# A node tile's eleven transposes put into one run on TensorE, between the products of n and those of z

## What is computed

```python
h = layernorm(x)
gi = segment_sum(edge_mlp(h[src], edge_attr), dst) @ W_ih.T + b_ih     # per node, from the edge stage
gh = h @ W_hh.T + b_hh                                                # 512 -> 3 * 512: r, z, n
r = sigmoid(i_r + h_r); z = sigmoid(i_z + h_z)
n = tanh(i_n + r * h_n)
h_new = (1 - z) * n + z * h
x1 = x + h + batchnorm(h_new)
h2 = layernorm(x1)
f1 = h2 @ [Wg, W1 of 8 experts, Ws1] + biases                         # gate logits and hidden rows
hid = weight of the expert (0 unless in the top 2) * relu(f1)         # and the shared expert's
out = x1 + hid @ [W2, Ws2, biases]
```

## Time and profile before

| what | value |
|---|---|
| three runs | 1561.29, 1565.93, 1567.96 us, median 1565.93 |
| profiled execution | 1564.22 us, of which the span from first to last instruction is 1562.4 |
| TensorE busy | 1414.7 us, 91% of the span, 6780 products and transposes |
| VectorE busy | 1119.8 us, 72% |
| GpSimd busy | 935.3 us, 60% |
| ScalarE busy | 608.9 us, 39% |
| mean granted TensorE clock | 0.965 of full speed |

### The profile page before, as it was taken

One profiled execution on the slowest core, in us unless ns is written; L12 is line 12 of the kernel. 1 busy time (PEld: TensorE's weight loads), 2 busy tenths in 40 slices (PEclk: granted clock), 3 DMA queues, 4 the chain that ended last, 5 costly groups with the idle time before them and its releaser, 6 DMA issues. The chain is left out here.

```text
span 1562.4 us, 23252 instructions
## 1 busy us (share of the span) xinstructions
PE 1414.7 (91%) x6780; PEld 1143.0 (73%) x6780; DVE 1119.8 (72%) x2860; ACT 608.9 (39%) x1100; POOL 935.3 (60%) x1055
## 2 busy tenths in 40 slices
PE   4879988998355999999999999999999999999996
PEld 3658766786244787888888888788888888888884
DVE  4654333333124888888888888888888888888886
ACT  3421212112002444444444444444444444444442
POOL 3212221311116777778788777788777778877771
PEclk9979999999777999999999999999999999999998
DMA  6432243537432232233322222222222322232220
GB/s 184 161 142 74 59 109 69 119 78 190 114 86 78 88 100 94 98 99 100 101 95 96 93 94 94 95 94 97 97 98 98 98 98 98 98 98 98 96 85 30
DMA packets 77727, 156.00 MB, mean 100 GB/s; under 512 B 35937, under 2 KB 37839, under 8 KB 77569
## 3 DMA queue, kind: packets, MB, share of 16 engines
q0 software_dynamic: 45056, 79.03, 17.6%
q1 hardware_dynamic: 32638, 76.55, 15.1%
HBM read 103.38 MB, written 52.02 MB: 99 GB/s over the span
## 5 line engine op out<-in xcount | busy, mean ns | idle before, releaser
L1385 PE MATMUL bank<-whh_hi,h_hi 128*125 128x512 f32 x960 | 393.0, 409 | 31.4 <-DVE h_lo L480 31.4
L1385 PE MATMUL bank<-whh_hi,h_lo 128*125 128x512 f32 x960 | 380.7, 397 | 0.0
L1385 PE MATMUL bank<-whh_lo,h_hi 128*125 128x512 f32 x960 | 379.7, 395 | 0.0
L1385 PEld LDWEIGHTS bank<-whh_hi,h_hi 128*125 128x125 f32 x960 | 178.6, 186 | 69.8 <-DVE h_lo L480 31.8
L1385 PEld LDWEIGHTS bank<-whh_hi,h_lo 128*125 128x125 f32 x960 | 178.6, 186 | 45.3
L1385 PEld LDWEIGHTS bank<-whh_lo,h_hi 128*125 128x125 f32 x960 | 179.4, 187 | 38.1
L1152 POOL DMA_INDIRECT gates<-gates_in,slot_at x80 | 128.0, 1600 | 77.6 <-POOL slot_at L1150 69.4
L1239 ACT ACTIVATE hn_raw<-bank 125x512 f32<-125x512 f32 x80 | 47.8, 598 | 288.3 <-PE bank L1385 288.3
L1086 PE MATMUL bank<-wih_hi,a_hi 128*125 128x512 f32 x240 | 101.8, 424 | 49.7 <-DVE g_out L834 41.6
L506 POOL DMA_INDIRECT gates_in<-g_out,add_at x16 | 32.3, 2018 | 190.9 <-DVE g_out L834 111.8
L834 DVE SCALAR_TENSOR_TENSOR g_out<-ig_bias,is_first,bank 125x512 f32<-125x512 f32 x60 | 44.5, 746 | 135.6 <-PE bank L1086 78.7
(11 more groups left out here) (174 smaller groups left out, 3330.8 us busy)
## 6 DMA issues: line engine op xcount, KB each, us to landing
xt<-in_x SPq DMA_DIRECT2D x80, 250.0 KB
out<-y SPq DMA_DIRECT2D x80, 250.0 KB
gates_in<-g_out SPq DMA_DIRECT2D x20, 750.0 KB
gates_in<-ig_bias SPq DMA_DIRECT2D x5, 750.0 KB
wih_lo_raw<-in_wih_t SPq DMA_DIRECT2D x4, 768.0 KB, 11.0
whh_lo_raw<-in_whh_t SPq DMA_DIRECT2D x4, 768.0 KB, 15.4
gates<-gates_in,slot_at POOLq DMA_INDIRECT x80, 10.8
m_lo_raw<-in_attr_t SPq DMA_DIRECT2D x5, 250.0 KB, 5.2
```

Of the source, the lines that this page charges most:

```text
L1385: last = pe.matmul(to[0:R, :], a[:, s, k * R:(k + 1) * R], w[:, k, q * D:(q + 1) * D], start=n == 0, stop=n == 3 * DK - 1)
```

## The change

On TensorE the transposes of h2 and of hid move ahead of those of h, and all eleven stand between the last product of n and the first of z. The products of z are no longer split. On ScalarE the copy h_hi moves behind h2_hi and hid_hi, which is the new order of the transposes. Nothing else changes; counts of instructions are the same.

```diff
@@ scalar body
                     act.activation(r_gate[:, :], r_pre[:, :], ACT.Sigmoid).then_inc(r_done, 1)
-                if p.has(1):
-                    s = p.slot(1)
-                    act.wait_ge(h_turned, t + 2)
-                    wait_from(act, z_prod, t)
-                    act.activation(h_hi[:, s, :], b_th[:, 0:DK * R], ACT.Copy).then_inc(h_hi_done, 1)
                 if p.has(-1):
                     act.wait_ge(h2_turned, t)
...
                     act.activation(hid_hi[:, :], b_thid[:, 0:KF * R], ACT.Copy).then_inc(hid_hi_done, 1)
+                if p.has(1):
+                    s = p.slot(1)
+                    act.wait_ge(h_turned, t + 2)
+                    wait_from(act, z_prod, t)
+                    act.activation(h_hi[:, s, :], b_th[:, 0:DK * R], ACT.Copy).then_inc(h_hi_done, 1)
@@ tensor body
                     gate(s, b_n, 2).then_inc(n_prod, 1)
+                if p.has(-1):
+                    pe.wait_ge(h2_done, t)
+                    wait_from(pe, h2_lo_done, t - 1)
+                    turn(pe, b_th2, h2[:, p.slot(-1), :], DK).then_inc(h2_turned, 1)
+                if p.has(-2):
+                    pe.wait_ge(hid_done, t - 1)
+                    wait_from(pe, hid_lo_done, t - 2)
+                    turn(pe, b_thid, hid[:, p.slot(-2), :], KF).then_inc(hid_turned, 1)
                 if p.has(1) and not p.first(1):
                     turn_h(pe, p)
                 if p.has(0):
                     wait_from(pe, z_pre_done, t)
-                    gate(p.slot(0), b_z, 1, 0, 2)
-                if p.has(-1):
-                    pe.wait_ge(h2_done, t)
-                    wait_from(pe, h2_lo_done, t - 1)
-                    turn(pe, b_th2, h2[:, p.slot(-1), :], DK).then_inc(h2_turned, 1)
-                if p.has(0):
-                    gate(p.slot(0), b_z, 1, 2, DK).then_inc(z_prod, 1)
-                if p.has(-2):
-                    pe.wait_ge(hid_done, t - 1)
-                    wait_from(pe, hid_lo_done, t - 2)
-                    turn(pe, b_thid, hid[:, p.slot(-2), :], KF).then_inc(hid_turned, 1)
+                    gate(p.slot(0), b_z, 1).then_inc(z_prod, 1)
```

## The result

| | before | after |
|---|---|---|
| median of the runs | 1566.95 us (1561.29 to 1568.92) | 1709.43 us (1702.4 to 1711.36) |
| ratio to before, 95% interval | | 1.0908 [1.0865, 1.095] |
| profiled execution, its span | 1564.22, 1562.4 | 1710.4, 1708.6 |
| mean granted TensorE clock | 0.965 | 0.954 |

The changed kernel is 9% slower. The forecast was 1691, with a range of 1655 to 1730: the sign, the place and the mechanism held, and 19 us of the size were missed. The stretches of the changed kernel come first, in the columns of the earlier trace rows.

What follows compares the result with a forecast made beforehand. TensorE was taken to set the pace, paying every standstill in full. Waits for h2 and hid made the period 14.90 us against 13.30; 77 periods plus the ends added 127 to 1564.2, giving 1691 us, range 1655 to 1730.

Steps and rivals of the forecast that it cites:

- Part 1: On TensorE, three transpose runs become one: four changes of kind fall away, worth nothing; only f1's 0.38 us wait goes.
- Part 2: On TensorE behind n, h2's transposes wait until 1.36 us after hn_raw starts: 1.56 us of standstill a period.
- Part 3: On TensorE, hid's transposes wait 0.4 us more; VectorE ends hid 2.14 us after hn_raw starts, its copy meeting GpSimd's hn.
- The period: Time between two starts of hn_raw: 14.87 to 14.95 us, taken as 14.90, against 13.30 before.
- The lock of the gather: Gather beside VectorE's z_h_n: taken as zero; the rival, z_h_n held up to 1.4 us, 1800 us, had 4 in 100.
- the slip ahead of hn: VectorE's copy and subtraction come ahead of GpSimd's hn: period 14.48 us, total 1658 us, 12 in 100.
- a regularly caught cast: GpSimd's hn catches VectorE's cast ahead of the copy: 1719 us if every fourth period, 1804 if each; 14 in 100.
- The sum: 77 periods at 14.90 us add 123.5; with 1.6 for tile 79 and about 1.5 for tile 1, 1691 us.
- H+12.69: On ScalarE, the next hn_raw starts 12.69 us after H, the first transpose of hid on TensorE.
- the rival on the clock: TensorE's clock falls in the new gap: 5 us for half of a period's large products, near 2080 us, 3 in 100.

Runs made afterwards that it cites:

- first order of VectorE: Kernel before the change, with VectorE's steps of hid written, as a block, ahead of y: 1589.43 us, ratio 1.0112.
- second's: Kernel before the change, with VectorE's low halves of h and h2 put ahead of the first norm: 1577.35 us, ratio 1.0054.

## Why the prediction was right, and where it was off

**Part 1, the switches**: right. Worth nothing, shown by splitting a run, not only argued. The wait at f1 is gone, as said.

**Part 2, h2**: right. The transposes of h2 start at T+1.35, where T+1.36 was forecast. That standstill is paid in full was shown by covering it: 0.43 of ready work gave 0.43, 1.40 gave 1.38.

**Part 3, hid**: right, in its size and its cause. Hid is done at T+2.06 to T+2.20, copy and subtraction take 1.13 and 0.28 on average from 800 to 1700, 1.41 together (1.46 forecast), and with hn held back the 0.4 goes. The sign named for it, a wait of 0.3 to 0.5, does not show in TensorE's row of waits, which has 0.19 each (7.1 in 37): that row counts from the end of the run of four transposes. Counted from start to start the wait is 0.39 (800.52 to 801.34, less 0.43 for four transposes).

**The period**: 14.83 in the median, 14.90 forecast. **The lock of the gather**: zero, as taken. Neither the slip ahead of hn nor a regularly caught cast came; the cast was over 1 us long three times (tiles 2, 3 and 8).

**The sum**: 1710.4 for the profiled execution against 1691, by these terms over the 77 periods (145.6 where the sum has 123.5):

| term | us |
|---|---|
| ten half-clock periods, 165.2 in all against ten of 14.90 | +16.2 |
| the first two periods, 20.39 and 17.73 against 14.90 each | +8.3 |
| one period of 16.30, in which hid was caught twice (done at T+3.54) | +1.4 |
| the other 64, 949.8 in all against 14.90 each | -3.8 |
| together | +22.1 |

Half of the first two periods' 8.3 is hid's late end: by the prediction's H+12.69 they would take 17.8 and 16.2, 4.2 over. The other 4.1 is the clock again. So of the 22 us some 20 come from a low clock.

Outside the 77 periods the change cost 0.6 where 3.1 was forecast: tile 1's period is 3.4 longer and the end 3.1, but tile 1's hn_raw starts 5.9 earlier than before. Why that is so was not tried.

The step that was off is the rival on the clock. It was given 3 in 100 on the ground that the clock had stayed at 1.00 around one gap of 1.82, and it was priced as a case of its own, 5 us in every period, near 2080. One gap that did no harm is one sample: with 1.54 and 0.25 us of standstill the clock fell in 10 of 17 cases and not in the other 7, and in the first order of VectorE a single standstill of 1.92, close to that 1.82, brought it down in five of six. And the price was 1.6 us in 10 of the 77 periods, a term to add to the forecast and not a case of its own. The second term is one that rows already held: the earlier trace rows showed hid 1.45 late in tile 3, and a held subtraction in tile 8, where six products of z and more stood between. With that cover moved behind the transposes, the same lateness is paid by TensorE, and the sum should have taken these periods apart from the rest. That the result still lies in the range is in part luck: the upper end was drawn for a cast held in every third period, which did not come, and the clock, which did, was left out.

**What stays open**: why the clock falls at 10 of the 17 turns and not at the others with the same idle times, nor at the one with more, and why the loop's turn makes TensorE wait 0.15 longer for h2 and 0.08 for hid. One order was not tried, and it bears on the largest term: part 2 takes it as given that h2 stands behind hn_raw on ScalarE. In the ordinary period above GpSimd's shift, on which h2 waits, is over at T-0.80, while ScalarE stands idle for 4.45 us ahead of hn_raw. Whether h2 ahead of hn_raw would take most of the 1.55 away is open.

## What to carry to other kernels

On an engine that runs its list in order, a run of like operations stands where the latest operand of the run is ready, so before gathering operations ask for each when its operand is done, and count the wait for each as lost time where the ready work that covered it now stands behind: here 1.55 us for h2 and 0.4 for hid, 77 times. When the order of transposes on one engine changes, the list that evicts them must change with it on the next: 32 us hung on one copy that stood ahead of tanh. And where two engines hold each other up, look at which instruction starts first and by how much: moving hid's steps clear of hn, with the low halves reordered, gave the 2% that the run of eleven was never able to give.

## What the runs showed of the hardware

- TensorE's clock fell to about half behind 1.54 and 0.25 us of standstill with four transposes between, in 10 of 17 cases; it did not fall behind 1.39 and 0.17, nor behind 1.54 alone, nor in the one case of 1.54 and 1.61. It fell behind 1.39 and 1.46 (the second of the 77 periods) and, in the kernel with hid ahead of y, behind 1.92 alone in five of six cases. The length of the standstill alone does not decide it. I had expected nothing under the 1.82 of the earlier trace rows to matter. Useless products in the gap kept it up and made the kernel 13 us faster.
- GpSimd's hold on VectorE makes a period of two: when TensorE's wait is taken out, a period of 12.8 is followed by one of 14, since behind the shorter one hn comes ahead of the copy (0.13 in the first order) or of the cast (most of the second's). The mean (13.4 in the second order) is then no better than with the wait. Only a copy that is clear of hn, by 0.33 us in the row above (1011.76 to 1012.09), brings the full 0.4.
